# Identity products of TensorE at two stage ends and between the opening maximum products of two attentions

## The chip, the cores and the metric

The kernel runs on one core of one Trainium2 chip. The metric is the device time of one launch in microseconds (us), the median of several runs. The engines are named as in the profile: PE (TensorE, the matrix engine; PEld is its weight load), DVE (VectorE), ACT (ScalarE), POOL (GpSimd) and SP (SyncE, which issues most DMAs).

## The reference

Two transformer layers on 4 sequences of 1024 tokens with 256 channels, each step followed by a residual sum and a layer norm:

```python
x = L0_attn_x
x = _layernorm(x + _L0_attn_ref(x, ...), axis=-1)   # 16 heads of 16, normed q and k, rope, softmax
x = _layernorm(x + _L0_ffn_ref(x, ...), axis=-1)    # gated, hidden 768
x = _layernorm(x + _L1_attn_ref(x, ...), axis=-1)   # 8 heads of 32, causal, softmax
x = _layernorm(x + _L1_ffn_ref(x, ...), axis=-1)    # router, top 2 of 16 experts, 12 of them with matrices
return x
```

Both attentions need the maximum of each query's scores for the softmax:

```python
attn = jnp.einsum('bqhd,bkhd->bhqk', q, k)
attn = jax.nn.softmax(attn, axis=-1)
```

## The kernel before

The program has four stages, each a block in which every engine has its own hand-written instruction list; semaphores order them, and between two stages all engines meet twice in a barrier (L119, the block's end, shown below under the stage's own first line, and L103). Names of on-chip tensors begin with the stage's letter.

- Stage a, `phase_qkv0`: q, k and v of layer 0, tile by tile. At its end PE only turns the last tiles: four transposes of `y` (L279), a wait for ACT's copy of the turned tile, and one product with `neg` (L288), after which ACT copies once more (L339) and SP stores the result (L186).
- Stage b, `phase_attention0`. PE computes the scores twice. A first product of queries and keys (`max_product`, L848, 48 rows of the array, 512 columns) goes to one of four banks `PM` and DVE takes its row maxima (L994). The maxima are cut in two halves on POOL, turned by PE (`turn_max`, L861, into a corner of bank `PS[2]`), copied by ACT (L957) and put by SP's DMAs (L712) as two more rows beside the queries. The second product (`score`, L902, 50 rows, bank `PS[0]` to `PS[2]`) then has the maximum subtracted, ACT takes its exponential (L970), and `values` (L874) multiplies with v into `PO`, with all 128 rows. In steady work the maximum products of later steps alternate with the scores. Before the first score there are none to alternate with: the opening issues AHEAD = 24 steps of two maximum products alone, 38 of them before `turn_max(0)` and 10 after it.
- Stage c, `phase_ffn0`: projection, layer norm and feed-forward network of layer 0, and q, k, v of layer 1. The last work of PE is a group of products into `PO` (L1276) that ACT copies (L1414) and sends off (L1424). PE already has 16 identity products ahead of its last transposes (L1287, LAST_FILLS).
- Stage d, `phase_layer1`: attention of layer 1, router and experts. Its opening is like that of stage b: `max_product` (L2774) gives a pair of products with 96 rows and 128 to 512 columns each into one of two tiles `PM`, for eight of the twelve steps two small mask products on top (L2779), and DVE reduces the pair (L2958). Twelve steps (STEPS), `turn_max(0)` (L2785), six more steps (AHEAD) of the next group, then the scores (L2822), their exponentials (L2919), masks on POOL (L2874) and products with v (L2801).

Matrix products of two float32 operands, such as an identity product, appear in the trace as two records each, as do their weight loads; transposes and the products on `fp32r` data have one.

Of the kernel before, what the change touches and what calls it, by code (L numbers as in the profile page):

```python
# [14 lines left out]
P = 128  # L15
# [101 lines left out]
def phase_qkv0(nc, d, keep, stacks, shared):  # L117

    with ExitStack() as ctx:  # L119
# [41 lines left out]
        parts_out = [a.sem(f"parts_out{i}") for i in range(2)]  # L161
        v_out = [a.sem(f"v_out{i}") for i in range(4)]
        LAG = 3
        EARLY_PARTS = {(1, 1): "q", (2, 0): "k", (2, 1): "v"}
        block = ctx.enter_context(nc.Block())

# [76 lines left out]
        @block.tensor  # L243
        def _(pe):

            pe.wait_ge(centred, 1)

            def qk(b, t):
                n = b * TPB + t
                h, at = t // TPK, (t % TPK) * P  # L250
                if t % TPK == 0:
                    pe.wait_ge(x_in[h], b * 16 + 16)

                if not (first(b) and t < 2):
                    pe.wait_ge(z_done, n - 1)
                for c in range(CD):
                    mm = pe.matmul(QK[t % 2][:], xT[:, h, c, at:at + P], wT[:, c, 0:QK_COLS],
                                   start=(c == 0), stop=(c == CD - 1))
                mm.then_inc(qk_ready, 1)

            def values(b, t):
                n = b * TPB + t
                h, at = t // TPK, (t % TPK) * P

                if not (first(b) and t < 1):
                    pe.wait_ge(v_done, n)
                for c in range(CD):
                    mm = pe.matmul(V[:], xT[:, h, c, at:at + P], wT[:, c, QK_COLS:3 * DIM],
                                   start=(c == 0), stop=(c == CD - 1))
                mm.then_inc(v_ready, 1)  # L270

            def turn(b, t):
                n = b * TPB + t
                pe.wait_ge(y_done, n + 1)

                if not (first(b) and t < 2):
                    pe.wait_ge(lo_done, n - 1)
                for i in range(QK_BLK):
                    mm = pe.matmul(YT[t % 2][:, i], y[:, t % 4, i * P:(i + 1) * P], ident, is_transpose=True,  # L279
                                   start=(i == 0), stop=(i == QK_BLK - 1), skip_group_check=True)  # L280
                mm.then_inc(yt_ready, 1)

            def low(b, t):


                pe.wait_ge(hi_done, b * TPB + t + 1)
                high = parts[:, t // TPK, 0, :, (t % TPK) * P:(t % TPK + 1) * P]
                pe.matmul(YT[t % 2][:], neg[:], high, start=False, stop=True, skip_group_check=True).then_inc(turned_low, 1)  # L288

            def steps(b, lo, hi):  # L290
                for k in range(lo, hi):
                    if k < TPB:
                        qk(b, k)
                    m = k - 3
                    old = (b, m) if m >= 0 else (b - 1, m + TPB)
                    turns = (not first(b) or m >= 0) and m < TPB
                    if turns:
                        if first(b) and m == 0:
                            pe.wait_ge(const_in, 16)
                            pe.wait_ge(neg_set, 1)  # L300
                        turn(*old)
                    if k < TPB:
                        values(b, k)
                    if turns:
                        low(*old)

            pipeline(pe, steps, LAG)

        @block.scalar
        def _(act):  # L310
# [118 lines left out]
def first(b):  # L429

    return isinstance(b, int) and b == 0


def pipeline(eng, steps, lag):

    steps(0, 0, TPB)
    with eng.Fori(1, BATCH) as b:
        steps(b, 0, TPB)
    steps(BATCH, 0, 0) if lag == 0 else tail(steps, lag)
# [117 lines left out]
def phase_attention0(nc, d, keep, weights, stacks, shared):  # L557
# [17 lines left out]
    AHEAD = 24  # L575
    TURN_UNITS = [23, 55]
    LEAD = 3
    RING = 16
    SBANKS, MBANKS = 3, 4
    K = len(PAIRS1) * D0  # L580
# [84 lines left out]
    with ExitStack() as ctx:  # L665
# [168 lines left out]
        def _(pe):  # L834
# [4 lines left out]
            def max_product(g, x, kh, times=1):  # L839

                half, t, p, r = step_at(x)
                n, buf, first = (g * STEPS + x) * HALVES + kh, g % BUFS, half * BLK + t * P
                at = slice(r * ROWS0, r * ROWS0 + K)
                pe.wait_ge(max_taken, n + 1)
                for _ in range(times):
                    mm = pe.matmul(PM[n % MBANKS][:], qst[buf][at, p, first:first + P],  # L848
                                   kst[buf][at, p, kh * BLK:(kh + 1) * BLK], start=True, stop=True)
                mm.then_inc(max_scores, 1)  # L850

            def max_products(g, x):
                if x == 0:
                    pe.wait_ge(q_in[g % BUFS], (g // BUFS + 1) * turns)
                for kh in range(HALVES):
                    max_product(g, x, kh)

            def turn_max(u):

# [188 lines left out]
def block_pipeline(eng, step, lag):  # L1048

    for b in range(BATCH):  # L1050
        for h in range(HPS):
            step(b, h)
    for h in range(HPS, HPS + lag):
        step(BATCH - 1, h)
# [81 lines left out]
def phase_ffn0(nc, d, keep, weights, shared):  # L1136

    with ExitStack() as ctx:
# [41 lines left out]
        v_out = [a.sem(f"v_out{i}") for i in range(2)]  # L1180
        PREP = 2
        LAG = 2
        LAST_FILLS = 16
        block = ctx.enter_context(nc.Block())

        @block.sync
# [76 lines left out]
        def _(pe):  # L1263
# [101 lines left out]
                                lambda s, k: wdown[:, s, k, :], HC).then_inc(S["downed"], 1)  # L1365

            block_pipeline(pe, step, LAG)

        @block.scalar
        def _(act):  # L1370
# [1221 lines left out]
def phase_layer1(nc, d, keep, weights, tokens, shared):  # L2592
# [14 lines left out]
    DIAGONAL = [kt >= half * TPK for half, kt in ROUND_LIST]  # L2607
    PAIRED = 2
    AHEAD = 6
    TURN = 7  # L2610
    GAP = SBANKS
    TURN_PLACE = (TURN + 1) * G1
# [44 lines left out]
    with ExitStack() as ctx:  # L2657
# [102 lines left out]
        def _(pe):  # L2760
# [4 lines left out]
            def max_product(g, t, j):  # L2765

                qt, kh = STEP_LIST[t]
                w = keys(qt, kh)
                diagonal = kh == qt // TPK
                n = entry["max", g, t]  # L2770
                if j == 0:

                    pe.wait_ge(max_taken[n % MTILES], n // MTILES + 1)
                mm = pe.matmul(PM[n % MTILES][:, j, 0:w], qst[g % BUFS][0:K, j, qt * P:(qt + 1) * P],  # L2774
                               kst[g % BUFS][0:K, j, kh * BLK:kh * BLK + w], start=True, stop=not diagonal)
                if j == G1 - 1:
                    if diagonal:
                        for i in range(G1):
                            mm = pe.matmul(PM[n % MTILES][:, i, w - P:w], identb, mask_q, start=False, stop=True)  # L2779
                    mm.then_inc(max_scores, 1)  # L2780

            def turn_max(g):

                pe.wait_ge(m_cut, g + 1)
                pe.transpose(PT, mhalves[:].rearrange("p i m -> p (i m)"), ident).then_inc(m_turned, 1)  # L2785
# [53 lines left out]
            for t in range(STEPS):  # L2839
                for j in range(G1):  # L2840
                    max_product(0, t, j)
            turn_max(0)
            pe.wait_ge(q_in[1], Q_TURNS)
            for t in range(AHEAD):
                for j in range(G1):
                    max_product(1, t, j)

            pe.wait_ge(ones_set, BUFS)
            pe.wait_ge(m_copied, 1)
# [219 lines left out]
```

## Time and profile before

| | before |
|---|---|
| median of 3 runs | 1914.5 us (1914.3 to 1917.1) |
| time of the profiled execution | 1909.37 us |
| its span | 1907.4 us |
| PE busy | 1795.9 us, 94% |
| DVE busy | 1429.7 us, 75% |
| ACT busy | 1117.3 us, 59% |
| mean granted PE clock | 0.961 |

The span is the stretch from the first to the last instruction of the profiled execution; its own time is 2 us more. PEclk is the share of PE's full clock (2.4 GHz) that was granted; it is 1.00 or 0.50 at any moment. A busy PE is one with a record under way, and a record lasts longer than the product keeps the array, so that busy time alone does not tell whether PE is at its limit.

### The profile page before, as it was taken

The page shows a single profiled execution, that of the slowest core. Times are in us where ns is not written, and L with a number is a line of the kernel's source. Part 1 is how long each engine was busy: PE and PEld are TensorE (multiplying, and loading weights), DVE is VectorE, ACT ScalarE, POOL GpSimd, SP SyncE. Part 2 cuts the span into 40 slices and gives each one's busy share as a digit, 9 for nine tenths or more (in the row PEclk, how much of TensorE's full clock was granted, in tenths as well). Part 3 has the DMA queues.
Part 4 walks back from the last instruction along what each step waited for, and adds up shares of the span by engine and source line. Part 5 has one row for each costly group of instructions (what it writes and reads, how often), then busy time and mean ns, then how long its engine had stood idle before and what let it go on. Part 6 is the DMA issues. An engine that isn't in the chain of part 4 may idle for free. (4 is left out here: it accounts for less than half of the span.)

```text
span 1907.4 us, 34604 instructions
## 1 busy us (share of the span) xinstructions
PE 1795.9 (94%) x12690; PEld 1170.9 (61%) x12690; DVE 1429.7 (75%) x2814; ACT 1117.3 (59%) x2212; POOL 528.6 (28%) x686
## 2 busy tenths in 40 slices
PE   8989999999999999799999989999999987999994
PEld 4545444444444444388888865555555566999994
DVE  7879999999999999367677655466666554766665
ACT  4645888888888888622333214446463632655555
POOL 5760000233000001032223212212525243444444
PEclk9986999999999999899999988999999998999997
DMA  4883744565434502023444255546666334655555
GB/s 170 280 260 53 124 79 96 131 144 122 86 57 73 83 28 85 20 76 111 153 143 147 89 188 120 137 100 156 153 154 156 97 107 147 150 144 144 145 115 196
DMA packets 146600, 239.18 MB, mean 125 GB/s; under 512 B 25830, under 2 KB 81159, under 8 KB 146449
## 3 DMA queue, kind: packets, MB, share of 16 engines
q1 hardware_dynamic: 113312, 171.48, 36.8%
q0 software_dynamic: 17024, 34.25, 7.0%
q10 hardware_dynamic: 16112, 31.46, 4.5%
q8 instruction: 92, 1.51, 0.3%
q14 instruction: 60, 0.48, 0.1%
HBM read 137.49 MB, written 96.60 MB: 123 GB/s over the span
## 5 line engine op out<-in xcount | busy, mean ns | idle before, releaser
L994 DVE TENSOR_REDUCE b_mx<-b_PM 128x1 f32<-128x512 f32 x1024 | 621.0, 679 | 17.9 <-PE b_PM L848 17.5
L970 ACT ACTIVATE b_probs<-b_PS 128x512 f32<-128x512 f32 x1000 | 523.9, 606 | 69.1 <-PE b_PS L902 53.8
L848 PE MATMUL b_PM<-b_kst,b_qst 48*128 48x512 f32 x888 | 280.9, 430 | 0.0
L2919 ACT ACTIVATE d_probs<-d_PS 128x512 f32<-128x512 f32 (+3 forms) x384 | 166.5, 496 | 183.2 <-PE d_PS L2822 182.5
L902 PE MATMUL b_PS<-b_qst,b_kst 50*128 50x512 f32 x744 | 256.9, 436 | 2.1 <-issue 0.2
L2958 DVE TENSOR_REDUCE d_mx<-d_PM 128x2 f32<-128x1024 f32 (+1 forms) x192 | 179.9, 950 | 101.5 <-PE d_PM L2774 59.3
L902 PEld LDWEIGHTS b_PS<-b_qst,b_kst 50*128 50x128 f32 x744 | 120.4, 184 | 163.4 <-ACT b_probs L970 147.4
L2874 POOL TENSOR_SCALAR_AFFINE_SELECT d_probs<-d_probs 128x128 f32<-128x128 f32 x256 | 74.6, 305 | 268.1 <-ACT d_probs L2919 263.4
L790 POOL CAST b_mhalves<-b_maxima 128x16 fp32r<-128x16 f32 x32 | 6.3, 197 | 505.3 <-DVE b_maxima L1003 505.3
L848 PEld LDWEIGHTS b_PM<-b_kst,b_qst 48*128 48x128 f32 x888 | 142.0, 184 | 5.4
L874 PE MATMUL b_PO<-b_probs,x_v 128*32 128x384 f32 (+2 forms) x2048 | 145.2, 390 | 0.0
L874 PE MATMUL b_PO<-b_probs,b_vst 128*32 128x384 f32 (+3 forms) x1960 | 143.0, 397 | 1.0 <-ACT b_probs L970 0.9
L1257 POOL TENSOR_TENSOR c_hT<-c_hidden,c_hT 128x512 fp32r<-128x512 f32 x48 | 64.8, 1350 | 218.1 <-DVE c_hT L1504 218.1
L2562 DVE TENSOR_TENSOR f_h_low<-f_h,f_h_high 128x512 fp32r<-128x512 f32 x96 | 66.5, 692 | 72.8 <-ACT f_h_high L2352 72.8
L2822 PE MATMUL d_PS<-d_qst,d_kst 98*128 98x512 f32 (+3 forms) x288 | 106.3, 386 | 8.6 <-ACT d_probs L2919 4.1
L2385 POOL DMA_INDIRECT sums<-f_y,f_to x44 | 88.8, 2019 | 90.2 <-ACT f_y L2333 72.2
L848 PE MATMUL b_PM<-x_k,x_q 48*128 48x512 f32 x291 | 108.0, 508 | 3.0 <-DVEq L986 2.7
L2774 PE MATMUL d_PM<-d_kst,d_qst 96*128 96x512 f32 (+3 forms) x288 | 102.0, 372 | 3.0 <-DVE d_mx L2958 3.0
L902 PE MATMUL b_PS<-x_q,x_k 50*128 50x512 f32 x256 | 91.5, 448 | 0.6
L2822 PEld LDWEIGHTS d_PS<-d_qst,d_kst 98*128 98x128 f32 x288 | 53.9, 191 | 49.9 <-issue 32.5
L1276 PE MATMUL c_PG<-c_x1T,u_w_gate 128*128 128x512 f32 x288 | 76.7, 402 | 5.5 <-DVE c_hidden L1502 4.1
L2333 ACT ACTIVATE f_y<-f_y,f_coef 128x256 f32<-128x256 f32 x44 | 22.4, 510 | 95.2 <-DVE f_y L2540 95.2
(318 smaller groups left out, 3753.9 us busy)
## 6 DMA issues: line engine op xcount, KB each, us to landing
halves<-a_parts SPq DMA_DIRECT2D x7, 2048.0 KB, 8.7
qk<-c_halves ACTq DMA_DIRECT2D x7, 2048.0 KB
w_w<-L_ffn_fc1T SPq DMA_DIRECT2D x12, 1024.0 KB, 5.0
w_w<-L_ffn_fc2T SPq DMA_DIRECT2D x12, 1024.0 KB, 6.3
b_qst<-halves SPq DMA_DIRECT2D x72, 128.0 KB, 4.4
b_kst<-halves SPq DMA_DIRECT2D x72, 128.0 KB, 7.6
d_qst<-qk SPq DMA_DIRECT2D x36, 256.0 KB, 5.2
d_kst<-qk SPq DMA_DIRECT2D x36, 256.0 KB, 7.4
```

The costliest lines, as they stand in the source:

```text
L848: mm = pe.matmul(PM[n % MBANKS][:], qst[buf][at, p, first:first + P], kst[buf][at, p, kh * BLK:(kh + 1) * BLK], start=True, stop=True)
L874: mm = pe.matmul(PO[j * VS0:(j + 1) * VS0, cols], vst[g % BUFS][:, kt, j, :], probs[:, (R * G0 + i) % RING, cols], start=(kt == 0 and firs ...
L902: pe.matmul(score_bank(g, s)[:], kst[g % BUFS][at, p, kt * P:(kt + 1) * P], qst[g % BUFS][at, p, half * BLK:(half + 1) * BLK], start=True, ...
L970: act.activation(probs[:, s % RING], score_bank(g, s)[:], ACT.Exp).then_inc(exped, 1)
L994: dve.tensor_reduce(mx[:, half, (r * PAIRS0 + p) * TPH + t, kh:kh + 1], PM[n % MBANKS][:], AX.X, ALU.max)\
L1276: mm = pe.matmul(out, lhs(left, c), rhs(right, c), start=(k == 0 and c == 0), stop=(k == len(PAIRS1) - 1 and c == chunks - 1))
L2385: pool.indirect_dma_start(out=d["sums1"], out_offset=bass.IndirectOffsetOnAxis(ap=index.bitcast(U32), axis=0), in_=src, in_offset=None, bo ...
L2774: mm = pe.matmul(PM[n % MTILES][:, j, 0:w], qst[g % BUFS][0:K, j, qt * P:(qt + 1) * P], kst[g % BUFS][0:K, j, kh * BLK:kh * BLK + w], star ...
L2822: pe.matmul(PS[bank(s)][:, 0:w], kst[g % BUFS][0:KM, j, kt * P:(kt + 1) * P], qst[g % BUFS][0:KM, j, q0:q0 + w], start=True, stop=True).th ...
L2874: pool.affine_select(out=near, in_=near, pattern=[[1, P]], compare_op=ALU.is_ge, fill=0.0, base=0, channel_multiplier=-1)\
L2919: act.activation(probs[:, s % RING, 0:w], PS[bank(s)][:, 0:w], ACT.Exp).then_inc(exped, 1)
L2958: dve.tensor_reduce(mx[:, :, qt, kh], PM[n][:, :, 0:keys(qt, kh)], AX.X, ALU.max).then_inc(max_taken[n], 1)
```

## The change

A helper issues `count` products of the identity with itself into a bank that nothing reads. It is called at PE's end of stage a (8 products), at PE's end of stage c (8), after each of the 48 opening maximum products of stage b (1 each) and after each of the 18 opening steps of stage d (2 each): 100 products in all. No wait, semaphore, DMA or instruction of another engine is added or removed. Line numbers after the first edit move up by 1, after the helper by 9 and more.

```diff
@@ phase_qkv0
         LAG = 3
+        END_FILLS = 8
@@
             pipeline(pe, steps, LAG)
+            idle_products(pe, QK[0][:, 0:P], ident, END_FILLS)
@@
+def idle_products(pe, spare, ident, count):
+
+    for _ in range(count):
+        pe.matmul(spare, ident, ident, start=True, stop=True)
@@ phase_attention0
     LEAD = 3
+    LEAD_FILLS = 1
@@ max_products
                 for kh in range(HALVES):
                     max_product(g, x, kh)
+                    idle_products(pe, PS[0][:, 0:P], ident, LEAD_FILLS)
@@ phase_ffn0
-        LAST_FILLS = 16
+        LAST_FILLS, END_FILLS = 16, 8
@@
             block_pipeline(pe, step, LAG)
+            idle_products(pe, TR[0][:, 0:P], ident, END_FILLS)
@@ phase_layer1
     AHEAD = 6
+    LEAD_FILLS = 2
@@
             for t in range(STEPS):
                 for j in range(G1):
                     max_product(0, t, j)
+                idle_products(pe, PS[0][:, 0:P], ident, LEAD_FILLS)
             turn_max(0)
             pe.wait_ge(q_in[1], Q_TURNS)
             for t in range(AHEAD):
                 for j in range(G1):
                     max_product(1, t, j)
+                idle_products(pe, PS[0][:, 0:P], ident, LEAD_FILLS)
```

On PE, at the end of stage a and the start of stage b, the order before is this (L288 is the last product of stage a, the two branches are the block's ends, `b_PM` are the maximum products, `b_PS<-const` the turned maxima):

```order
L279 MATMUL a_YT<-const,a_y 128x128 x4
L288 MATMUL a_YT<-a_parts,a_neg 128x512
L119 UNCONDITIONAL_BRANCH
L833 UNCONDITIONAL_BRANCH
L848 MATMUL b_PM<-x_k_50,x_q_49 128x512 x38
L861 MATMUL b_PS<-const,b_mhalves 128x128
L848 MATMUL b_PM<-x_k_50,x_q_49 128x512 x10
L902 MATMUL b_PS<-x_q_49,x_k_50 128x512
```

The same place of the changed kernel, as far as the first maximum products; L439 is the helper, and the pair of L857 and L439 goes on in this way 48 times:

```order
L280 MATMUL a_YT<-const,a_y 128x128 x4
L289 MATMUL a_YT<-a_parts,a_neg 128x512
L439 MATMUL a_QK<-const 128x128 x8
L119 UNCONDITIONAL_BRANCH
L842 UNCONDITIONAL_BRANCH
L857 MATMUL b_PM<-x_k_50,x_q_49 128x512
L439 MATMUL b_PS<-const 128x128
```

The eight products at the end of stage a stand ahead of PE's branch to the barrier, and the runs of 38 and 10 maximum products have become single ones with an identity product behind each.

On PE, at the end of stage c and the start of stage d in the changed kernel (L1286 is the last real product of stage c, L2786 and L2791 are the maximum and mask products of the first steps):

```order
L1286 MATMUL c_PO<-u_w_qkv,c_x2T 128x256 x24
L439 MATMUL c_TR<-const 128x128 x8
L1148 UNCONDITIONAL_BRANCH
L2771 UNCONDITIONAL_BRANCH
L2786 MATMUL d_PM<-x_k_61,x_q_60 128x128 x2
L2791 MATMUL d_PM<-d_fixed 128x128 x2
L439 MATMUL d_PS<-const 128x128 x2
L2786 MATMUL d_PM<-x_k_61,x_q_60 128x256 x2
```

All L439 rows are new; the others stood next to each other before.

## Rows read from the trace of the kernel before

**Rows 1.** The page: span, and the granted clock in 40 equal slices

```profile
span 1907.4 us, 34604 instructions
PEclk9986999999999999899999988999999998999997
```

**Rows 2.** Windows around stage a's end and stage b's opening (busy us, records, PEclk)

```profile
120.00:124.00 4.00, 1.16 (x5) 0.60 (x5) 3.02 (x6) 2.23 (x5) 3.08 (x3) 1.00 1.03 386
131.60:152.00 20.40, 20.03 (x36) 9.61 (x36) 19.55 (x33) 0.00 (x0) 6.77 (x11) 0.50 0.91 144
163.60:167.40 3.80, 3.80 (x17) 2.83 (x14) 3.80 (x8) 2.73 (x6) 0.00 (x0) 0.50 0.01 2
167.40:173.40 6.00, 6.00 (x37) 2.31 (x36) 3.24 (x6) 2.42 (x6) 0.00 (x0) 0.54 0.01 3
173.40:188.00 14.60, 14.52 (x155) 6.83 (x154) 14.39 (x25) 13.11 (x27) 0.42 (x2) 1.00 0.44 64
```

**Rows 3.** Timeline, stage a's end and barrier (start us, us, engine, work)

```profile
126.43 1.06 PE L279 MATMUL a_YT<-const,a_y 128*128 128x128 f32 x4
128.17 0.79 PE L288 MATMUL a_YT<-a_parts,a_neg 128*128 128x512 f32 x1 [0.69 <-ACT a_parts L337]
129.63 0.36 SPq L186 DMA_DIRECT2D halves<-a_parts  x1
131.66 1.23 PE L848 MATMUL b_PM<-x_k,x_q 48*128 48x512 f32 x4 [2.69 <-DVEq L986]
```

**Rows 4.** Timeline, stage b's opening and first scores

```profile
134.99 0.28 PEld L848 LDWEIGHTS b_PM<-x_k,x_q 48*128 48x128 f32 x1 [0.31 <-DVE b_mx L994]
136.65 15.62 DVE L994 TENSOR_REDUCE b_mx<-b_PM 128x1 f32<-128x512 f32 x26
153.74 0.47 PE L861 MATMUL b_PS<-const,b_mhalves 128*128 128x128 f32 x1
159.59 0.62 PE L902 MATMUL b_PS<-x_q,x_k 50*128 50x512 f32 x1
160.25 4.67 ACT L970 ACTIVATE b_probs<-b_PS 128x512 f32<-128x512 f32 x8 [4.43 <-PE b_PS L902]
165.23 0.62 PE L902 MATMUL b_PS<-x_q,x_k 50*128 50x512 f32 x1
165.65 0.62 PE L902 MATMUL b_PS<-x_q,x_k 50*128 50x512 f32 x1
170.50 1.93 PE L874 MATMUL b_PO<-b_probs,x_v 128*32 128x128 f32 x16
```

**Rows 5.** Source L1287, the identity products that are there before

```profile
L1287 PE MATMUL c_PG<-const x32: 272/275/275, 1108.7 to 1112.2; 128*128 128x128 f32 x32
```

**Rows 6.** Timeline, stage c's end and stage d's start

```profile
1124.23 0.39 PE L1276 MATMUL c_PO<-u_w_qkv,c_x2T 128*128 128x256 f32 x2
1125.07 0.37 ACTq L1424 DMA_DIRECT2D v<-c_vaug  x1
1127.39 0.44 PE L2774 MATMUL d_PM<-x_k,x_q 96*128 96x128 f32 x2 [2.77 <-DVE d_mhalves L2950]
```

**Rows 7.** DVE in stage d's opening, 1127.3 to 1142.2, by form

```profile
L2958 DVE TENSOR_REDUCE d_mx<-d_PM 128x2 f32<-128x1024 f32 x6 | 7.2, 1222 | 2.4 <-PE d_PM L2774 2.1 <-PE d_PM L2779 0.2
```

**Rows 8.** Windows of stage d's start

```profile
1129.00:1142.00 13.00, 10.23 (x32) 5.86 (x30) 10.01 (x11) 0.00 (x0) 7.03 (x4) 0.50 0.69 163
1142.00:1148.80 6.80, 5.76 (x23) 3.99 (x24) 4.63 (x9) 1.55 (x2) 0.00 (x0) 0.50 0.41 93
1148.80:1154.90 6.10, 6.10 (x25) 4.86 (x22) 3.85 (x5) 3.50 (x8) 2.28 (x8) 0.50 1.02 249
1159.20:1163.00 3.80, 3.80 (x26) 2.72 (x25) 2.99 (x6) 2.68 (x6) 0.00 (x0) 0.98 0.01 2
```

**Rows 9.** Timeline, what PE did ahead of two other rises of the clock

```profile
1154.89 3.26 PE L2801 MATMUL d_PO<-d_probs,x_v 128*64 128x512 f32 x8
808.39 2.76 PE L1276 MATMUL c_PU<-c_x1T,u_w_up 128*128 128x512 f32 x6
```

## The prediction

> **What bounds the kernel now.** I read the page's clock row first, then windows of 2 to 4 us wherever it is below nine, then the timeline there. The kernel is one chain of stages, and work lost at a stage's start is lost at the end of the program. The clock row dips in four places [rows 1]; two are the ones this change touches. At the end of stage a PE has little to do: 1.16 us busy of 4 [rows 2]. Behind that stretch the clock is at 0.50 through the whole opening of stage b and beyond it, to about 173.4, where it comes up [rows 2]. The second stretch is stage d's start: 0.50 from 1129 to 1154.9, and 0.98 from 1159.2 on [rows 8].
>
> What sets the pace in these stretches? In stage b's opening it is DVE, not PE. DVE is busy 19.55 of 20.40 us [rows 2], its 26 takes in 15.62 us are one each 0.60 us, and PE's weight load waits 0.31 us for a free bank each time [rows 4]. From the first maximum product at 131.66 to the first score at 159.59 are 27.9 us for 48 products [rows 3, 4], which is 48 times 0.60 less the last few that the scores overtake. The first eight scores still go at the pace of ACT, 4.67 us for eight or 0.58 each [rows 4]. Only from about 165 does the half clock bind. In stage d's opening the half clock does bind: DVE sits idle 2.4 us ahead of its six widest takes [rows 7], and after 1148.8 PE is busy all the time while DVE and ACT are not [rows 8].
>
> **What an identity product costs.** The 32 records of 16 products start between 1108.7 and 1112.2 [rows 5], 3.5/31 = 0.113 us apart at clock 1.00, so 0.226 us for a product. At 0.50 the nearest row is four transposes of the same shape in 1.06 us [rows 3]; less one record's latency of about 0.38 that leaves 0.227 us each, two of them 0.45 us; twice the row at full clock, less its small fixed part, gives 0.43. I take 0.44. A maximum product at 0.50 takes 0.42 us of the array: scores follow each other at 165.23 and 165.65 [rows 4], one maximum product beside each in the other rows of the array. At 1.00 it takes half, 0.21.
>
> **Stage a's end: 8 products.** PE's last product ends at 128.17 + 0.79 = 128.96, SP's last issue at 129.99, and the next stage's first product starts 1.67 us later [rows 3]. Eight products at the half clock are 8 x 0.44 = 3.5 us, so PE comes to the barrier at 132.5, 2.5 us later than SP did. Part of the 1.67 us is SP's own way from its last issue to the barrier, for which I take off 0.3 (an estimate between 0 and 0.6), so the next stage starts 2.2 us late, at 133.9. If the clock rises among these products it is 1.4 (half of them at 0.226). Cost 1.4 to 2.5 us, I take 2.2. The cover that is there (1 us until SP arrives) is used up.
>
> **Stage b's opening: 48 products.** It hangs on the clock. At 1.00 a maximum product and an identity product are 0.21 + 0.23 = 0.44 us, under DVE's 0.60: hidden, cost nothing. At 0.50 they are 0.42 + 0.44 = 0.86 us, over it: PE becomes the bound and 48 of them take 41.3 us in place of 27.9. Cost 13.4. The turned maxima don't hide it: they come after 38 products, 32.7 us in, and their rows need 159.59 - 153.74 = 5.9 us [rows 4], while the ten pairs behind need 8.6.
>
> So is the clock up? Three things decide it. First, does it rise during the eight products: they are as dense as PE's work gets, and I think it mostly does. Second, does it then survive the barrier, in which PE is idle for 1.6 us (the 1.67 less SP's share, with the latencies of PE's own last and first product), right behind a burst of only about 3 us. Stage c's end lost the clock after an idle stretch of 1124.62 to 1127.39, 2.8 us, though long dense work preceded it [rows 6]. 1.6 us behind little work is between that and nothing; I give it a third. Third, once at 0.50, do the pairs of the opening lift it? In the trace before, PE was without a pause from 163.6 to 167.4 at 0.50, and the clock didn't move [rows 2]: scores and maximum products there use 48 and 50 rows. 6.1 us of products with 96 and 98 rows, PE always busy, didn't lift it either [rows 8]. The rises came behind runs of products over all 128 rows: sixteen with v in 1.93 us at 170.50 [rows 4], eight in 3.26 us at 1154.89, six at 808.39 [rows 9]. A cold opening is half 48-row products and half full ones; it is nearer to the mixed stretches that did not rise, and it is the same mixture for 41 us, so that it either rises early or not at all. I take not at all.
>
> The Trainium skill says in TensorE: Matmul & The Clock Gate (Part 1: The HAM clock gate) that "the default state is throttled, and activity releases the throttle". Read simply, a PE kept busy throughout the opening must be warm; the trace agrees for full-height products and not for the short ones at 163.6. By the page the 13.4 us would be near 0; it stands below as a rival.
>
> **What a full clock would bring in stage b.** In the opening nothing, it is DVE's. Behind it, ACT works 2.73 + 2.42 = 5.15 us in the 9.8 us from 163.6 to 173.4, against 13.11 of 14.6 in steady work [rows 2], at which pace it would need 5.7: at most 4.1 us. The first eight scores gain nothing from it, and in them PE has even less to do at 1.00 than in the stretches behind which the clock fell, so I expect 0.7 of it, and only if the opening is warm. In the likeliest case: nothing.
>
> **Stage c's end: 8 products.** The clock is 1.00 there. PE ends at 1124.62, plus 8 x 0.226 = 1.8 gives 1126.4; ACT's last issue ends at 1125.44 [rows 6]. The barrier is 0.8 to 1.0 us later, I take 0.9.
>
> **Stage d's opening: 36 products.** The idle stretch over the barrier shrinks from 2.8 to about 1.9 us, and the pairs are full of large products: at 0.50 a 1024-wide step is 2 x 0.42 + 2 x 0.44 = 1.7 us against DVE's 1.22 [rows 7], at 1.00 it is 0.87, hidden. Here more than half of PE's time is full-height work and the rest 96 rows, so I expect the clock to be up most of the time, lost once (over the barrier, or where PE waits for the turned maxima) and back within a few us. Gains at a full clock: 2.4 in the opening (DVE's idle time), 0.8 of the 6.8 us to the first score (DVE works 4.63 of them [rows 8], and the identity products take part of the slack), and of the 10.4 us from 1148.8 to 1159.2 half of the 3.26 us with v (1.6) and some 1.2 of the 6.1 before (ACT and DVE are busy 3.50 and 3.85 of them). Sum 6.0. From it goes a stretch of some 3.5 us with the half clock, in which the added products cost 0.44 each for about four steps, 1.8. Net 4.2, less the barrier's 0.9: 3.3 us gained. Bounds: 5.1 with no cold stretch, and -6 if all of it were cold (24 x 0.44 = 10.6 more in the twelve steps against 3 of slack, the rest likewise, still bounded by a later rise).
>
> **The sum.** 2.2 + 13.4 - 3.3 = 12.3 us more. The profiled execution took 1909.4 us at a span of 1907.4; it would be 1921.7. The median of the runs shown is 5.1 above it, so 1926.8, and I say **1926**.
>
> **The rivals.**
> - *The clock comes up ahead of stage b's opening and holds.* For it: the eight products are dense, the idle time is only 1.6 us, and afterwards an identity product each 0.6 us. Then 1.4 - 0.7 - 3.3 = -2.6, down to 1.4 - 4.1 - 5.1 = -7.8: 1907 to 1913, likeliest 1911. It ends on the other side; it decides at one point, whether the clock is 1.00 at the second maximum product. Chance 0.25.
> - *The cold opening warms up by itself, as the page's rule would have it.* Each cold microsecond costs 0.3 us (0.86 against 0.60), so a rise after 5 to 20 us leaves 1.5 to 6 us of the 13.4: 2.2 + 4 - 3.3 = +3, 1914 to 1920, likeliest 1917. Against it the rows with a busy PE and no rise. Chance 0.13.
> - *Stage d is cold too.* Its pairs cost more than they bring: 12.3 + 3.3 + 6 = 21 or more, 1932 to 1940. Chance 0.07.
> - The forecast, a cold opening in b and a mostly warm one in d: 1921 to 1932. Chance 0.55.
>
> **How the numbers follow.** The 80% range leaves out stage d cold and the better end of the first rival: 1910 to 1931. A measurement can tell 0.2%, 3.8 us, from no change. Faster than 1910.7 is somewhat over half of the first rival, 0.15, and a little for bounds of d that are too narrow: 0.17. Within 1910.7 to 1918.3 are the rest of it and half of the second: 0.19. Slower: 0.64.
>
> **What would show it.** Windows: PEclk 0.50 from about 124 to 170 and more in stage b, with the first score near 175 and PE, not DVE, without idle time ahead of it; DVE waiting for each `b_PM`. The takes of DVE 0.86 us apart. The first product of stage b near 133.9. In stage d, takes of 1.22 us back to back, PEclk 1.00 in most of the first 20 us, and the products with v twice as fast as the 3.26 us of before [rows 9]. The prediction is wrong if DVE's takes stay 0.60 apart in stage b (first or second rival), or if the clock rises by half-height products.

## The result and the profile after

| | before | after |
|---|---|---|
| median | 1915.8 us (4 runs, 1914.3 to 1920.9) | 1953.5 us (4 runs, 1950.6 to 1958.1) |
| ratio | | 1.0194 (95%: 1.0164 to 1.0224) |
| profiled execution | 1909.37 us | 1950.56 us |
| span, mean clock | 1907.4 us, 0.961 | 1948.6 us, 0.960 |

The kernel is 1.9% slower, 41 us of span where the forecast had 12, and outside the range. The page of the changed kernel, first its head, then PE's row and the clock in 40 slices:

```profile
span 1948.6 us, 35004 instructions
PE 1837.2 (94%) x12890; PEld 1201.0 (62%) x12890; DVE 1434.6 (74%) x2814; ACT 1116.6 (57%) x2212; POOL 531.7 (27%) x686
...
PEclk9975799999999999989999999999999997999998
```

Against [rows 1] the dip near slice 3 has become deeper and longer, and the two dips at slices 24 and 25, where stage d starts, are gone. The mean clock says nothing of either: it is the same.

To find where the 41.2 us of span come from, I took the start of each stage in both traces. Timeline of the changed kernel, PE's rows at the stage starts and ends:

```profile
134.17 0.76 PE L857 MATMUL b_PM<-x_k,x_q 48*128 48x512 f32 x1 [1.26 <-DVEq L996]
...
203.79 0.79 PE L912 MATMUL b_PS<-x_q,x_k 50*128 50x512 f32 x1
203.80 0.79 PE L857 MATMUL b_PM<-x_k,x_q 48*128 48x512 f32 x1
...
836.79 0.62 PE L1286 MATMUL c_PO<-u_w_proj,x_att2T 128*128 128x256 f32 x3 [2.75 <-DVEq L1460]
...
1168.84 1.95 PE L439 MATMUL c_TR<-const 128*128 128x128 f32 x16
1172.57 0.44 PE L2786 MATMUL d_PM<-x_k,x_q 96*128 96x128 f32 x2 [1.78 <-DVE d_mhalves L2964]
```

- Stage b starts at 134.17 instead of 131.66 [rows 3]: +2.5.
- The first score is at 203.79 instead of 159.59 [rows 4]. From the first maximum product that is 69.6 us in place of 27.9: **+41.7**.
- Stage c starts 43.5 us late (before: 793.33), so the rest of stage b gives 0.7 back.
- Stage d starts at 1172.57 instead of 1127.39 [rows 6], 45.2 late: +0.9 inside stage c, +0.8 at its end.
- The end is 41.2 late, so stage d gains 4.0.

Each of these is read from one profiled execution of each kernel. Kernels whose stage d is the one before (that kernel and experiments 2 to 5, 7 and 9) take 780.0 to 788.6 us from its first product to the end, and the rest of stage b, the same instructions in all of them, takes 630.9 to 634.8 us. The +41.7 stands far above that scatter; -0.7, +0.9 and -4.0 do not.

One place holds the whole loss. Windows of the changed kernel there and at stage d's start (busy us and records of PE, PEld, DVE, ACT, POOL, then the granted clock, DMA share, GB/s):

```profile
134.10:150.00 15.90, 15.83 (x33) 8.63 (x33) 7.48 (x11) 0.00 (x0) 6.79 (x11) 0.50 0.99 136
150.00:203.80 53.80, 53.80 (x115) 29.15 (x114) 25.75 (x39) 1.55 (x2) 0.41 (x2) 0.50 0.01 2
203.80:216.00 12.20, 12.20 (x62) 6.64 (x63) 9.30 (x16) 7.70 (x15) 0.00 (x0) 0.50 0.00 1
216.00:230.00 14.00, 14.00 (x153) 6.55 (x155) 13.20 (x23) 11.95 (x24) 0.42 (x2) 0.99 0.36 54
1172.50:1186.00 13.50, 12.28 (x88) 10.21 (x88) 11.20 (x14) 0.00 (x0) 7.04 (x4) 1.00 0.71 175
1186.00:1192.00 6.00, 5.54 (x45) 4.88 (x46) 4.35 (x7) 1.55 (x2) 0.00 (x0) 1.00 0.34 80
```

In stage b's opening PE is busy 53.80 of 53.80 us and DVE only 25.75: PE has become the bound, as forecast. But an array that works 0.86 us for a pair, as the prediction had it, should be through with 48 pairs in 41 us. The timeline of one pair shows what is missing:

```profile
138.48 0.79 PE L857 MATMUL b_PM<-x_k,x_q 48*128 48x512 f32 x1
139.20 0.50 PEld L439 LDWEIGHTS b_PS<-const 128*128 128x128 f32 x2 [0.44 <-issue]
139.20 0.80 PE L439 MATMUL b_PS<-const 128*128 128x128 f32 x2
139.31 0.69 DVE L1004 TENSOR_REDUCE b_mx<-b_PM 128x1 f32<-128x512 f32 x1 [0.76 <-PE b_PM L857]
139.93 0.28 PEld L857 LDWEIGHTS b_PM<-x_k,x_q 48*128 48x128 f32 x1 [0.23 <-issue]
139.93 0.79 PE L857 MATMUL b_PM<-x_k,x_q 48*128 48x512 f32 x1
```

From one maximum product to the next are 139.93 - 138.48 = 1.45 us, not 0.86, and 48 times 1.45 are the 69.6. By the prediction's prices the maximum product holds the array 0.42 us, but the identity product behind it starts 0.72 us after it; the identity product holds it 0.44, and the next maximum product starts 0.73 us after it. So each time 0.3 us pass in which, by these prices, the array takes nothing new, though the PE row shows no pause: a record lasts 0.79 us and the next one starts 0.72 us after it. It shows in the weight loads: they are idle 0.44 and 0.23 us for "issue", for nothing that the profile knows. The waits from 134 to 204 sum this up (total us, times, longest us):

```profile
DVE b_mx L1004 <- PE b_PM L857: 46.6, 48, 11.0
PEld b_PS L439 <- issue: 21.0, 48, 0.4
PEld b_PM L857 <- issue: 11.9, 47, 1.5
```

What differs between the two products is the shape of the array. A maximum product takes 48 rows of one half of the array, and the other half is free for a neighbour: behind the opening a score and a maximum product start together (203.79 and 203.80). The identity product takes all 128 rows. The theory that the runs below test: **going from half-array to whole-array products, or back, costs 0.30 us at the half clock**. Why it would is a guess: the new weights wait until the array has run empty. The trace of before had the hint. Its timeline, at the one place of the opening where a 128-row product stands among 48-row ones:

```profile
154.14 5.65 PE L848 MATMUL b_PM<-x_k,x_q 48*128 48x512 f32 x10
```

`turn_max` started at 153.74 [rows 4], 0.72 us behind the maximum product ahead of it (153.02), as in the pairs. It is one record of 128 columns, and the next maximum product comes 0.40 us later. An identity record of the same shape is through the array in about 0.21 us at this clock, so this way back cost 0.19 us, not 0.30.

### The profile page after: what moved, and what is told of

It is laid out like the page before. It is cut to its first block and busy times, and to the rows that moved or that the text cites. A ratio compares the mean times of both kernels' runs of the same rounds, so it can differ in the third digit from the quotient of the medians.

```text
span 1948.6 us, 35004 instructions
## 1 busy us (share of the span) xinstructions
PE 1837.2 (94%) x12890; PEld 1201.0 (62%) x12890; DVE 1434.6 (74%) x2814; ACT 1116.6 (57%) x2212; POOL 531.7 (27%) x686
## 5 line engine op out<-in xcount | busy, mean ns | idle before, releaser
L857 PE MATMUL b_PM<-b_kst,b_qst 48*128 48x512 f32 x888 | 281.0, 430 | 0.0
L857 PEld LDWEIGHTS b_PM<-b_kst,b_qst 48*128 48x128 f32 x888 | 141.9, 184 | 5.2
L857 PE MATMUL b_PM<-x_k,x_q 48*128 48x512 f32 x291 | 118.0, 507 | 1.3 <-DVEq L996 1.3
L2786 PE MATMUL d_PM<-d_kst,d_qst 96*128 96x512 f32 (+3 forms) x288 | 98.2, 358 | 3.6 <-DVE d_mx L2972 3.6
L2834 PEld LDWEIGHTS d_PS<-d_qst,d_kst 98*128 98x128 f32 x288 | 53.5, 189 | 47.2 <-issue 32.3
L1286 PE MATMUL c_PG<-c_x1T,u_w_gate 128*128 128x512 f32 x288 | 76.7, 402 | 5.5 <-DVE c_hidden L1513 4.1
L912 PEld LDWEIGHTS b_PS<-x_q,x_k 50*128 50x128 f32 x256 | 43.8, 192 | 56.7 <-ACT b_probs L980 50.0
```

What stands on the lines that cost most here:

```text
L912: pe.matmul(score_bank(g, s)[:], kst[g % BUFS][at, p, kt * P:(kt + 1) * P], qst[g % BUFS][at, p, half * BLK:(half + 1) * BLK], start=True, ...
L2834: pe.matmul(PS[bank(s)][:, 0:w], kst[g % BUFS][0:KM, j, kt * P:(kt + 1) * P], qst[g % BUFS][0:KM, j, q0:q0 + w], start=True, stop=True).th ...
```

## The experiments

Their edits are given against the changed kernel, and the lines that take out other calls are not shown. Only experiment 1 keeps all the other identity products. Experiments 2 to 5 and 9 have those of stage b's opening alone (5 has 20 more), 6, 11 and 12 those of stage d's opening alone, 7 the two stage ends, 8 and 10 what they name. What an identity product writes is never read; every kernel here still computes all of the reference. Each median is compared with runs of the kernel before made at the same time (medians 1910.9 to 1912.4 us), which is why 1914.5 us can be a ratio near 1. "Start to first score" is from the stage's first maximum product to its first score: before, 27.9 us in stage b and 21.4 in stage d (1127.4 to 1148.8).

**1. Without stage b's 48 products**

```diff
-                    idle_products(pe, PS[0][:, 0:P], ident, LEAD_FILLS)
```

> The changed kernel without the 48 identity products in stage b's opening; the end products and stage d's stay. Theory 1 (all of the loss is stage b's opening, 41.7 of the 43.5 us by which stage c starts late): first score of stage b about 28 us after the first maximum product, the opening at DVE's 0.60 us, total near before + 2.5 (stage a's end) + 0.9 (stage c's end) - 5 (stage d) = within 3 us of before, 1912 to 1917. Rival (the end products or stage d carry a part of the loss): over 1920.

Measured: 1914.5 us, ratio 1.0000 (0.9984 to 1.0016). The whole loss goes with the one line. The other 52 products together change nothing that can be told from the noise.

**2. Stage b's 48 products alone** (the other four calls removed)

> The kernel before with only the 48 identity products of stage b's opening. Theory 1 (each costs two changes between products on one half of the array's rows and products on all of them, 0.3 us each at the half clock, beside the 0.44 of the product itself): a pair every 1.45 us, first score 69 to 70 us after the first maximum product, total before + 41 to 42. Rival (the late and cold end of stage a matters): a pair of another length, or the clock up within the opening.

Measured: 1955.8 us, ratio 1.0228 (1.0201 to 1.0256); start to first score 69.6 us, the same as in the changed kernel. The 2.2 us of the eight products ahead are not needed for it.

**3. Identity products on the same rows as their maximum product**, in stage b alone: 48 rows of the identity, into the bank that goes with that half of the array

```diff
-                    idle_products(pe, PS[0][:, 0:P], ident, LEAD_FILLS)
+                    r = step_at(x)[3]
+                    idle_products(pe, (PS[0], PO)[r][:, 0:P], ident[r * ROWS0:r * ROWS0 + K], LEAD_FILLS)
```

> As the one before, but each identity product uses the 48 rows of the maximum product ahead of it (a 48-row slice of the identity, into a bank of its own for each half of the rows), so that the array's division stays the same. Theory 1 (change of division): the extra 0.59 us goes, a pair every 0.75 to 0.86 us, first score 36 to 42 us after the first maximum product, total before + 9 to + 14. Rival (two-pass float32 identity products behind a one-pass product cost 1 us wherever they stand): still 1.45 us and + 41.

Measured: 1914.2 us, ratio 1.0012 (0.9995 to 1.0029); start to first score 29.3 us. As many products, as many columns, the same clock: window over the opening and, from the timeline, DVE's takes.

```profile
132.00:161.00 29.00, 28.81 (x144) 27.47 (x145) 27.48 (x47) 1.55 (x2) 7.18 (x13) 0.50 0.63 106
```

```profile
136.84 16.22 DVE L1004 TENSOR_REDUCE b_mx<-b_PM 128x1 f32<-128x512 f32 x27
```

The clock is 0.50, and still DVE sets the pace, 16.22 / 27 = 0.60 us a take. So the 42 us are not the work of the identity products: they are their shape. It was even cheaper than I thought (29.3 us, where 36 to 42 were expected): the two halves work at the same time, so that 0.42 + 0.44 us of one half fit under 0.60.

**4. The same 48 identity products in lumps of eight**, which leaves 12 changes of shape instead of 96

```diff
-                    idle_products(pe, PS[0][:, 0:P], ident, LEAD_FILLS)
+                if x % 4 == 3:
+                    idle_products(pe, PS[0][:, 0:P], ident, 8 * LEAD_FILLS)
```

> The same 48 full identity products, but eight together behind every eight maximum products: 12 changes of division in place of 96. Theory 1: at the half clock a group takes 8 x 0.42 + 8 x 0.44 + 0.6 = 7.5 us, six of them 45 us, total before + 16, less if the runs of eight raise the clock (then 8 x 0.60 for DVE bound groups, before + 2 to + 8). Rival (1 us for each identity product wherever it stands): 8 x 0.42 + 8 x 1.0 = 11.6 us a group, before + 41.

Measured: 1929.6 us, ratio 1.0079 (1.0047 to 1.0111); start to first score 44.6 us. PE's timeline:

```profile
132.08 1.23 PE L856 MATMUL b_PM<-x_k,x_q 48*128 48x512 f32 x4 [2.53 <-DVEq L996]
...
136.13 3.78 PE L438 MATMUL b_PS<-const 128*128 128x128 f32 x16
139.84 0.93 PE L856 MATMUL b_PM<-x_k,x_q 48*128 48x512 f32 x4
```

The first eight products and their lump take 7.76 us where eight pairs take 11.6, with the same array work at the same clock. What is left over 8 x 0.60 is another cost: for the 3.7 us of a lump DVE has at most four full banks to take. The clock rose behind the first two lumps (at 140.3 and 147.1) and fell again after the maximum products behind them (143.7 and 150.5). That a risen clock would leave only 2 to 8 us was a miss: the mean clock of this opening is 0.65, and it still costs 16.6 us.

**5. A warm start**: 20 identity products ahead of stage b's opening, then the 48 pairs

```diff
+            idle_products(pe, PS[0][:, 0:P], ident, 20)
```

> The kernel before with the 48 full identity products of stage b's opening and 20 more ahead of its first maximum product, so that the clock is up when the pairs begin. Theory 1 (every change of division waits until the array has run empty, also at full clock): a pair takes 0.44 us of the array and 2 x 0.15 to 0.3 us of changes, 0.75 to 1.0 us, over DVE's 0.60, so that even a warm opening is PE's and lasts 36 to 48 us; with 6 to 9 us for the 20 ahead, before + 15 to + 30. Rival (the prediction's price, 0.44 us a pair at full clock, hidden under DVE): takes of DVE 0.60 us apart and before + 6 to + 9.

Measured: 1956.8 us, ratio 1.0217 (1.0196 to 1.0238). This looks at the pair at the full clock and tests my first rival. PE's timeline, a pair at 1.00 and, 4 us on, one at 0.50:

```profile
132.07 6.85 PE L438 MATMUL b_PS<-const 128*128 128x128 f32 x40 [2.54 <-PEq L103]
...
140.53 0.50 PE L856 MATMUL b_PM<-x_k,x_q 48*128 48x512 f32 x1
140.95 0.49 PE L438 MATMUL b_PS<-const 128*128 128x128 f32 x2
141.37 0.50 PE L856 MATMUL b_PM<-x_k,x_q 48*128 48x512 f32 x1
...
144.25 0.79 PE L856 MATMUL b_PM<-x_k,x_q 48*128 48x512 f32 x1
145.70 0.79 PE L856 MATMUL b_PM<-x_k,x_q 48*128 48x512 f32 x1
```

A pair takes 0.84 us at the full clock where the array's work is 0.21 + 0.23 = 0.44: the change of shape is 0.20 us there. So even a warm opening would have been over DVE's 0.60. And it did not stay warm, so the 36 to 48 us expected for the pairs became 66.4, and the total was missed. The clock was 1.00 when the pairs began at 138.85. PE was busy for all of the next 4.55 us, yet it fell at 143.4, for 75 us, and PE stayed busy for all of the 61.8 us to the first score.

**6. Stage d's 36 products alone**

> The kernel before with only the 36 identity products of stage d's opening. Theory 1 (they raise the clock within the opening, since 96-row and 128-row products need no change of division): clock up by about 6 us into the opening, first product with the output weights (beginning of the routing work) 3 to 6 us early, and of it 0 to 3 us left at the end. Rival (they need the end products of stage c to hold the clock): half clock until the first products with v, as before, and a total of before + 3 to + 8.

Measured: 1911.2 us, ratio 0.9986 (0.9971 to 1.0000). Windows from stage d's start to its first score:

```profile
1127.00:1142.50 15.50, 13.90 (x88) 11.61 (x88) 11.53 (x15) 0.00 (x0) 7.03 (x4) 0.89 0.66 170
1142.50:1148.30 5.80, 5.76 (x48) 5.11 (x48) 4.23 (x5) 1.55 (x2) 0.00 (x0) 1.00 0.32 82
```

The clock comes up, as forecast, and it brings little: 21.2 us to the first score where before had 21.4 at 0.53. The first product with layer 1's output weights comes 125.5 us after the start instead of 132.0 (128.2 to 133.5 in the profiles with stage d as before), and by the end no gain is left that the profile could show: stage d takes 784.2 us, before 780.0.

**7. The two stage ends alone**

> The kernel before with only the 8 + 8 identity products at the ends of stages a and c. Both theories: the barriers come 2.2 and 0.9 us later, and what the clock gives back is little without the products behind: before + 1 to + 3.

Measured: 1917.4 us, ratio 1.0029 (1.0014 to 1.0045). The eight products at stage a's end run at the half clock for 3.58 us, and stage b starts at 134.0. The clock comes up at 132.5, is 1.00 over the barrier and falls at 136.0; windows on both sides:

```profile
134.00:135.90 1.90, 1.28 (x6) 0.53 (x6) 1.38 (x3) 0.00 (x0) 1.10 (x3) 1.00 0.15 56
136.00:160.00 24.00, 24.00 (x42) 11.37 (x42) 24.00 (x42) 1.55 (x2) 6.00 (x11) 0.50 0.64 87
```

They bought 2 us of full clock in a stretch that DVE bounds, for 2.4 us of delay. With 0.8 at stage c's end the two delays are 3.2 us. The medians are 5.0 apart, more than the 1 to 3 expected; 3.2 is within the interval, which is 2.7 to 8.6 us.

The clock over this barrier isn't the same each time: it came up at the end of these eight products here and in experiment 1 (1.00 from 132.0 to 135.4), and in the changed kernel's profile it stayed at 0.50 from 124.1 to 216.3.

**8. Stage d's 36 products and the eight at stage c's end**

> The kernel before with the 8 identity products at the end of stage c and the 36 of stage d's opening. Theory 1: the clock holds over the barrier, stage d runs at full clock from its start, 5 to 8 us gained by the first product with the output weights; if the later half of stage d is set by its own chain, 0 to 4 us of it are left at the end, else all of it: before - 5 to 0.

Measured: 1910.8 us, ratio 0.9991 (0.9972 to 1.0011). Now stage d's opening has the full clock from its start, and the output weights come 122.8 us after it, 9 us sooner than before. It did not last. Windows of this kernel and of the kernel before over the same piece of stage d, from one group of products with v to another (the counts of records show that the work is the same):

```profile
1289.70:1310.70 21.00, 20.80 (x93) 13.29 (x91) 7.97 (x19) 7.55 (x17) 2.15 (x7) 0.67 0.34 100
```

```profile
1298.20:1312.90 14.70, 14.52 (x94) 9.61 (x91) 7.93 (x19) 7.35 (x17) 2.16 (x7) 1.00 0.37 113
```

The clock fell at 1294.9 in the run of this kernel, with PE busy 5.00 of the 5.20 us before it in this window, and stayed at 0.50 for 13.7 us, with PE busy throughout. The piece takes 21.0 us in place of 14.7, and the kernel's lead of 8.5 us over the one before shrinks to 2.2. Why it falls there and not before isn't settled. Dips of 3 to 14 us lie elsewhere in stage d in each kernel's profile, so a lead of a few us in one profile is not yet a gain.

**9. Experiment 3 with twice the work**: two identity products on 64 rows behind each maximum product, in stage b alone

```diff
-    LEAD_FILLS = 1
+    LEAD_FILLS = 2
...
-                    idle_products(pe, PS[0][:, 0:P], ident, LEAD_FILLS)
+                    r = step_at(x)[3]
+                    idle_products(pe, (PS[0], PO)[r][:, 0:P], ident[r * ROWS0:(r + 1) * ROWS0], LEAD_FILLS)
```

> The kernel before with two identity products behind each of stage b's 48 opening maximum products, on the same half of the array's rows (64 rows) and with a bank for each half, so that there is no change of division and the halves work at the same time. Theory 1: at the half clock each half of the rows has 2.55 us of work in DVE's 2.4 for four products, so the array is nearly full, the clock comes up within the opening, and the opening stays at DVE's 0.60: 28 to 30 us. What a warm opening then brings (the prediction said 0.7 us, bounded by 4.1): before - 4 to + 1. Rival (products on half the rows never raise the clock, however many): half clock to 173 as before, opening 1 to 3 us longer, before + 1 to + 3.

Measured: 1933.5 us, ratio 1.0125 (1.0104 to 1.0146); start to first score 47.2 us. My theory missed this one twice. I had both halves of the array busy, and thought that this would bring the clock up. It did not:

```profile
132.00:162.00 30.00, 29.90 (x156) 28.35 (x157) 21.37 (x31) 0.00 (x0) 6.79 (x11) 0.50 0.63 100
162.00:179.30 17.30, 17.30 (x88) 15.87 (x88) 11.70 (x19) 1.55 (x2) 0.41 (x2) 0.50 0.01 2
```

And at 0.50 the 0.42 + 2 x 0.44 = 1.30 us of one half take 0.94 us in the mean (two maximum products start every 1.88 us, at 150.29 and 152.17): the halves overlap in part only. With a full overlap it would be 0.65, and still over DVE's 0.60.

**10. Experiment 9's stage b with stage c's end and stage d's opening**

> The same in stage b, with the 8 identity products at the end of stage c and the 36 of stage d. The sum of both: the gain of stage b's opening, if any, and the 0 to 2 us that stage d's kept: before - 6 to 0. If the two do not add, a later chain takes back what the first gave.

Measured: 1929.9 us, ratio 1.0090 (1.0063 to 1.0117). A miss, for experiment 9's reason: stage b's start to first score is 47.2 us again.

**11. The change of shape, put where it was not**: stage d's 36 products on 64 rows instead of 128, which is less work for the array (the same edit in both loops)

```diff
-                idle_products(pe, PS[0][:, 0:P], ident, LEAD_FILLS)
+                idle_products(pe, PS[0][:, 0:P], ident[0:P // 2], LEAD_FILLS)
```

> The kernel before with only the 36 identity products of stage d's opening, but each on 64 rows, so that stage d now has the change of division that stage b had: 36 changes in 18 steps. Theory 1: 0.2 us a change at the full clock and 0.3 at the half, and half the height to raise the clock: the step of two 512-wide products takes 0.85 + 0.85 + 0.6 = 2.3 us at the half clock against DVE's 1.22, first score 10 to 20 us later than with full-height ones, before + 8 to + 20. Rival (a change costs only where 48-row products are concerned): as with the full-height ones, within 3 us of before.

Measured: 1937.6 us, ratio 1.0130 (1.0107 to 1.0154), so 1.4% over experiment 6. A 1024-wide step in the timeline:

```profile
1137.69 1.22 PE L2783 MATMUL d_PM<-x_k,x_q 96*128 96x512 f32 x2
1138.84 0.93 PEld L438 LDWEIGHTS d_PS<-const 64*128 64x128 f32 x4 [0.65 <-issue]
1138.84 1.22 PE L438 MATMUL d_PS<-const 64*128 64x128 f32 x4
...
1139.99 0.50 PEld L2783 LDWEIGHTS d_PM<-x_k,x_q 96*128 96x128 f32 x2 [0.23 <-issue]
```

The step takes 1139.99 - 1137.69 = 2.30 us. Two products of 0.42 and two of 0.44 are 1.72; the rest is 0.58, twice 0.29. The clock stayed at 0.50 for 47.8 us, where experiment 6 had 3.4, and the first score came 41 us after the start. The total is 26.7 us over before, past the 8 to 20 expected, and holds the lost clock as well as the changes; the step's own time, at one clock, shows the changes alone. This is the strongest of the runs for the theory: fewer rows, and slower, by the same 0.3 us at each of the two places.

But 0.30 us is not the price of every change. In the steps with masks the identity products stand behind a 128-column mask product. Here, and in experiment 6 at the same clock, where the shape stays whole:

```profile
1140.48 0.44 PE L2788 MATMUL d_PM<-d_fixed 128*128 128x128 bf16 x2
1140.85 1.22 PE L438 MATMUL d_PS<-const 64*128 64x128 f32 x4
```

```profile
1128.87 0.44 PE L2788 MATMUL d_PM<-d_fixed 128*128 128x128 bf16 x2
1129.10 1.17 PE L438 MATMUL d_PS<-const 128*128 128x128 f32 x4
```

From the masks to the identity products are 0.37 us with the change and 0.23 without, so it costs 0.14. The way back, to the next maximum product, is 1.15 against 0.82 us, so it costs 0.33.

**12. Stage d with one identity product a step instead of two**

```diff
-    LEAD_FILLS = 2
+    LEAD_FILLS = 1
```

> The kernel before with one full-height identity product in place of two behind each of stage d's 18 opening steps, and nothing else. Theory 1 (96-row products, masks and one identity product are still dense enough to raise the clock, with less added work): first product with the output weights 3 to 8 us early as with two, and most of it given back before the experts: before - 4 to + 1. Rival (one is not enough, the clock stays at half until the products with v): before, within 1 us, and the first score no earlier than 21 us after the stage's first product.

Measured: 1911.2 us, ratio 0.9997 (0.9981 to 1.0013). Its clock is 0.86 as far as `turn_max` and falls at 1143.7. The first score comes 22.0 us after the start, the output weights 129.3, not the 3 to 8 us early that were expected:

```profile
1129.20:1144.50 15.30, 12.03 (x67) 9.24 (x67) 11.53 (x15) 0.00 (x0) 7.03 (x4) 0.86 0.67 172
1144.50:1151.30 6.80, 6.80 (x35) 5.68 (x34) 3.89 (x5) 1.55 (x2) 0.00 (x0) 0.55 0.59 137
```

No kernel here is clearly faster than the one before; the best, experiment 6, is 0.14% below it, with an interval that touches 1.

## Why the prediction was wrong

The step that failed is the price of a pair in stage b's opening: "at 0.50 they are 0.42 + 0.44 = 0.86 us". The mechanism was right (clock at 0.50, PE over DVE's pace, the cost lands on the span), the size was not. A pair takes 1.45 us, which is 0.42 + 0.44 and twice 0.30, and the term is +41.7 us, not +13.4. I priced an instruction by its time in a run of its equals [rows 3, 4, 5], and took pairs of unlike products to cost the sum. Experiments 3, 4 and 11 show that the missing part belongs to the change of shape: no change, no cost; fewer changes, less; changes at another place, 0.14 to 0.33 us each there. The Trainium skill says it in TensorEngine Tiling (Array Packing), Tiling Modes, Key Properties: "Mode switching requires drain". The traces agree in that each change takes time in which no product starts, and the runs give it its price, in these pairs 0.30 us each way at the half clock and 0.20 at the full one. That the array runs empty meanwhile, no row shows. I had not weighed that rule.

The other steps:

- **Stage a's end**, +2.2: measured +2.5, the upper bound. Over all profiles stage b starts at 131.7 to 132.3 without these products and at 133.7 to 134.2 with them. Right. That the clock mostly rises among the eight did not hold in the changed kernel's profile; it did at the end of them in two others.
- **The cold opening does not warm up**: right, for 70 us. The rule of the Trainium skill in TensorE: Matmul & The Clock Gate (Part 1: The HAM clock gate), that activity releases the throttle, would have had the clock up, and the trace disagrees if a busy PE is meant: 53.80 of 53.80 us busy at 0.50. In the changed kernel nothing new starts in 0.6 of each 1.45 us, which could be why; but experiment 9 has no change of shape among its pairs and was not lifted either, in 47.2 busy us.
- **The first rival, a warm opening**, at 0.25: the worst misjudgement of chances. Experiment 5 shows that it could not have paid. Its pair, 0.44 us by my sum, is 0.84 us, over DVE's 0.60, and the clock falls among such pairs. With the price right, every case of mine would have been slower than before.
- **Stage c's end**, +0.9: +0.8, and the same 0.8 in experiments 1, 7 and 8. Right.
- **Stage d**, gross gain 4.2: 4.0 in this profile. The mechanism held for the start: no low clock from the stage's start to 1387, DVE's idle time ahead of the wide takes down from 2.4 to 0.9 us, products with v twice as fast. The after rows that answer to [rows 7] and [rows 9], DVE by form and PE's timeline:

```profile
L2972 DVE TENSOR_REDUCE d_mx<-d_PM 128x2 f32<-128x1024 f32 x6 | 7.2, 1223 | 0.9 <-PE d_PM L2786 0.7
```

```profile
1196.27 1.72 PE L2813 MATMUL d_PO<-d_probs,x_v 128*64 128x512 f32 x8
```

  But the route was not mine. The first score came only 1.8 us sooner, the output weights 8.3 us sooner (123.7 after the start, before 132.0), and then half of it was lost later. That my number fits is luck. The gain at the output weights can be told from the scatter (122.8 to 125.9 us after the start in the five profiles with both identity products a step on 128 rows, 128.2 to 133.5 in those with stage d as before). At the end it can't: stage d takes 776.0 to 784.2 us in the former and 780.0 to 788.6 in the latter, and experiments 6 and 8, with 12 runs each, are within noise of before. In stage d the identity products have all 128 rows, and the maximum products' 96 rows are more than half an array, so there is no change of shape to pay. The timeline shows an identity product 0.24 us behind a 512-column maximum product at 1176.67, when its array time is 0.21.
- **Not priced**: -0.7 in the rest of stage b, +0.9 within stage c. I have no cause for them; both are within the scatter between profiles (630.9 to 634.8 us for the one; 333.0 to 335.0 for stage c, without the products at its end).

The sum 2.5 + 41.7 - 0.7 + 0.9 + 0.8 - 4.0 = 41.2 us is the difference of the spans.

## What to carry to other kernels

Before you put a product between others, compare how much of the array each one takes. If one takes half or less and the other more, each change cost 0.14 to 0.33 us here at the half clock, 0.30 in the pairs that made the loss and 0.20 for them at the full one, and the PE row shows no gap for it; look for weight loads that wait for "issue". Fill with products of the same shape; if that can't be, fewer and longer lumps pay for fewer changes, though experiment 4 shows that a lump also starves the engine that reads the results.

And before you pay for TensorE's clock, ask which engine sets the pace of the stretch that would get it. Here DVE did in stage b's opening, and in stage d's the full clock brought the first score 1.8 us sooner at best; even the versions that have the clock up at little cost (experiments 6 and 8) move the end by 0.1%, which is within the noise.

## What the hardware showed that I had not expected

- The change between half-array and whole-array products: in the pairs 0.30 us at 1.2 GHz and 0.20 us at 2.4 GHz, so it doesn't simply double with the clock's period. At 1.2 GHz it was only 0.14 behind a 128-column mask product and 0.19 behind `turn_max`, so it depends on what stands ahead.
- Two halves of the array do overlap when they are fed in turn: 0.86 us of work in each fit under a 0.60 us pace (experiment 3), 1.30 us took 0.94 (experiment 9).
- The clock fell at 143.4 in experiment 5 after 4.55 us in which PE was busy without a pause, and at 1294.9 in experiment 8 after 5.00 busy us of 5.20. A busy PE row is no promise of a full clock.
- The same eight products at the same barrier raised the clock in two profiles and left it at 0.50 in a third, so one profile doesn't settle where a rise comes.
